# A gate projection split into four groups and placed inside the attention loop of a fused linear-attention layer on Trainium2

## The reference

```python
xn = _layernorm(x, axis=-1)                      # per token, 2048 features
q, k, v = xn @ Wq + bq, xn @ Wk + bk, xn @ Wv + bv
qf, kf = elu(q) + 1, elu(k) + 1                  # 16 heads of 128
# chunks of 128 tokens: kv and ksum of all earlier chunks are a running state
out = (qf @ kv_state + causal(qf @ kf.T) @ v) / (z_inter + z_intra + EPS)
s = out @ Wo + bo
g = silu(_layernorm(xn) @ ternary(W))            # the "f" projection
y = x + s * g
```

## Time and profile before

| what | us |
|---|---|
| runs shown | 4029.22 and 4381.51, median 4205.36 |
| the profiled execution | 4017.58 |
| its span, first to last instruction (core 3) | 4016.1 |
| PE busy | 2907.0 (72%) |
| DVE busy | 1137.6 (28%) |
| ACT busy | 1035.4 (26%) |

### The profile page before, as it was taken

One profiled execution on the slowest core, in us unless ns is written; L12 is line 12 of the kernel. 1 busy time (PEld: TensorE's weight loads), 2 busy tenths in 40 slices (PEclk: granted clock), 3 DMA queues, 4 the chain that ended last, 5 costly groups with the idle time before them and its releaser, 6 DMA issues.

```text
span 4016.1 us, 43354 instructions; the slowest of 8 cores (3976.9 to 4016.1 us)
## 1 busy us (share of the span) xinstructions
PE 2907.0 (72%) x15876; PEld 1535.7 (38%) x15876; DVE 1137.6 (28%) x1469; ACT 1035.4 (26%) x1200; POOL 218.6 (5%) x268
## 2 busy tenths in 40 slices
PE   1244545686969598777969597768959696859876
PEld 1011112443453344434444345434444345334443
DVE  4222363313231322313140322232141323232222
ACT  2010101412333132313232133313241233313221
POOL 2233112000000000000000000000000000000000
PEclk8676767797979698788979798879979797979888
DMA  5888867154404542254404542254404541344223
GB/s 190 273 290 283 295 227 243 40 154 170 152 31 128 171 152 95 63 158 165 152 22 138 172 153 71 89 174 152 131 30 150 178 153 37 123 134 152 95 79 129
DMA packets 225227, 581.81 MB, mean 145 GB/s; under 512 B 26240, under 2 KB 26336, under 8 KB 200448
## 3 DMA queue, kind: packets, MB, share of 16 engines
q1 hardware_dynamic: 198144, 436.30, 34.7%
q0 software_dynamic: 26880, 142.74, 10.1%
HBM read 503.43 MB, written 75.50 MB: 144 GB/s over the span
## 4 chain that ended last, share of the span: by engine, by line
PE 60%; DMA 13%; DVE 11%; issue 8%; ACT 5%; POOL 1%; DVEq 0%; SPq 0%; ACTq 0%; POOLq 0%
PE psA L492 51%; DMA wsc<-pcast 6%; DVE xn2T L455 3%; DMA y<-xres 3%; DMA wring<-wsc 3%; DVE kvbf L661 2%; ACT scr L634 2%; ACT scr L639 2%; DMA xres<-x 1%; PE psB L608 1%; PE psB L431 1%; PE psB L614 1%; PE psB L437 1%; PE psA L580 1%; DVE lst L349 1%
## 5 line engine op out<-in xcount | busy, mean ns | idle before, releaser
L492 PE MATMUL psA<-xnT,wring 128*128 128x512 bf16 x6144 | 1435.5, 399 | 381.5 <-DMA wring<-wsc 341.7
L492 PEld LDWEIGHTS psA<-xnT,wring 128*128 128x128 bf16 x6144 | 621.1, 102 | 1193.5 <-issue 538.8
L492 PE MATMUL psA<-xn2T,wring 128*128 128x512 bf16 x2048 | 478.3, 399 | 113.6 <-DVE ksumst L675 63.9
L492 PE MATMUL psA<-qat,wring 128*128 128x512 bf16 x2048 | 443.3, 379 | 0.0
L492 PEld LDWEIGHTS psA<-xn2T,wring 128*128 128x128 bf16 x2048 | 207.3, 102 | 382.1 <-issue 163.3
L723 DVE TENSOR_TENSOR xnT<-scr,vg 128x512 bf16<-128x512 f32 x128 | 88.6, 692 | 805.3 <-ACT scr L715 805.3
L492 PEld LDWEIGHTS psA<-qat,wring 128*128 128x128 bf16 x2048 | 200.4, 98 | 241.6
L431 PE MATMUL psB<-identb_s,xns 128*128 128x128 bf16 x512 | 59.7, 310 | 231.1 <-DVE xn2T L455 137.2
L507 ACT ACTIVATE scr<-psA,bs_q 128x512 f32<-128x512 f32 x128 | 88.0, 687 | 488.0 <-PE psA L492 482.4
L516 DVE SCALAR_TENSOR_TENSOR qat<-scr 128x512 bf16<-128x512 f32 x128 | 88.6, 692 | 418.5 <-ACT scr L510 418.5
L536 ACT ACTIVATE vg<-psA,bs_v 128x512 bf16<-128x512 f32 x128 | 88.0, 687 | 452.8 <-PE psA L492 452.8
(11 more groups left out here) (97 smaller groups left out, 2529.2 us busy)
## 6 DMA issues: line engine op xcount, KB each, us to landing
wring<-wsc SPq DMA_DIRECT2D x1280, 256.0 KB, 2.7
wsc<-pcast POOLq DMA_DIRECT2D x160, 256.0 KB, 8.1
xln<-x POOLq DMA_DIRECT2D x32, 1024.0 KB, 7.2
xres<-w_f SPq DMA_DIRECT2D x32, 1024.0 KB, 6.5
xres<-x POOLq DMA_DIRECT2D x32, 1024.0 KB, 8.1
y<-xres POOLq DMA_DIRECT2D x32, 1024.0 KB, 7.2
xres<-w_q SPq DMA_DIRECT2D x16, 1024.0 KB, 7.5
xres<-w_k SPq DMA_DIRECT2D x16, 1024.0 KB, 7.6
```

The lines of the kernel that those rows point to most:

```text
L492: op("tensor", lambda e, k=k, ti=ti, bk=bk, rb=rhs_buf: e.matmul(psA[:, bk * 512:(bk + 1) * 512], wring[k % NRING][:, (ti % 8) * 128:(ti % ...
```

## The change

The body of `proj_phase` becomes `proj_tile`, and the f projection is no longer a stage of its own: tiles 4j to 4j+3 are computed at the end of chunk j of the attention loop. As `vg` still holds v there, Silu writes the gate into `xnT`, and the product of stage 6 goes from `xnT` into `vg`. Layer norm A of the next super-chunk now stands behind the last f tile. No instruction is added or removed in the code.

```diff
+            def proj_tile(m, to, evac_fn, rhs_buf, rhs_deps):
...
             def proj_phase(m, evac_fn, rhs_buf, rhs_deps):
                 for to in range(NT):
+                    proj_tile(m, to, evac_fn, rhs_buf, rhs_deps)
...
+            def evac_f(to, bk, pe_n):
+                wait("scalar", s_pe, pe_n)
+                op("scalar", lambda e, to=to, bk=bk: e.activation(
+                    xnT[:, to * T:(to + 1) * T], psA[:, bk * 512:(bk + 1) * 512],
+                    AF.Silu), [(s_ac, 1)])
+                psA_bank_rel[bk] = (s_ac, s_ac.n)
...
                 set_rel("a_m", (s_pe, pe_io))
+                for to in range(4 * j, 4 * j + 4):
+                    proj_tile("f", to, evac_f, xn2T,
+                              [(s_ac, ac_ln_done)])
+            f_done_ac = s_ac.n
             attn_dv_done = s_dv.n
...
             if sc + 1 < nsc:
                 emit_ln_A(sc + 1, attn_dv_done)
-
-            def evac_f(to, bk, pe_n):
-                wait("scalar", s_pe, pe_n)
-                op("scalar", lambda e, to=to, bk=bk: e.activation(
-                    vg[:, to * T:(to + 1) * T], psA[:, bk * 512:(bk + 1) * 512],
-                    AF.Silu), [(s_ac, 1)])
-                psA_bank_rel[bk] = (s_ac, s_ac.n)
-
-            proj_phase("f", evac_f, xn2T, [(s_ac, ac_ln_done)])
-            f_done_ac = s_ac.n
...
                 op("vector", lambda e, to=to, ssl=ssl: e.tensor_tensor(
-                    xnT[:, to * T:(to + 1) * T], scr[:, ssl[0]:ssl[1]],
-                    vg[:, to * T:(to + 1) * T], ALU.mult), [(s_dv, 1)])
+                    vg[:, to * T:(to + 1) * T], scr[:, ssl[0]:ssl[1]],
+                    xnT[:, to * T:(to + 1) * T], ALU.mult), [(s_dv, 1)])
...
-                        xnT[:, t * T + j * 128: t * T + (j + 1) * 128],
+                        vg[:, t * T + j * 128: t * T + (j + 1) * 128],
...
-            set_rel("xnT", (s_pe, s_pe.n))
+            set_rel("xnT", (s_dv, sg_dv_done))
+            set_rel("vg_next", (s_pe, s_pe.n))
```

More of the change, by code:

```diff
@@ L467, in build_nc @@
             dv_ln_done, ac_ln_done = emit_ln_B(sc)
+            def proj_tile(m, to, evac_fn, rhs_buf, rhs_deps):
+                kA, wnA = stream_whalf(m, to, 0)
+                kB, wnB = stream_whalf(m, to, 1)
+                bk = to % 4
+                r0 = psA_bank_rel[bk]
+                if r0 is not None:
+                    wait("tensor", r0[0], r0[1])
+                if to == 0:
+                    for sem, cnt in rhs_deps:
+                        wait("tensor", sem, cnt)
+                wait("tensor", wnA[0], wnA[1])
+                for ti in range(NT):
+                    k = kA if ti < 8 else kB
+                    incs = []
+                    if ti == 0 and pending_wfree[0]:
+                        incs = [(s_wfree, pending_wfree[0])]
+                        pending_wfree[0] = 0
+                    if ti == 8:
+                        incs = [(s_wfree, 1)]
+                        wait("tensor", wnB[0], wnB[1])
+                    if ti == NT - 1:
+                        incs = [(s_pe, 1)]
+                    op("tensor", lambda e, k=k, ti=ti, bk=bk, rb=rhs_buf: e.matmul(
+                        psA[:, bk * 512:(bk + 1) * 512],
+                        wring[k % NRING][:, (ti % 8) * 128:(ti % 8 + 1) * 128],
+                        rb[:, ti * T:(ti + 1) * T],
+                        start=(ti == 0), stop=(ti == NT - 1)), incs)
+                pending_wfree[0] += 1
+                evac_fn(to, bk, s_pe.n)
+                pump(2)
@@ L469, in proj_phase @@
             def proj_phase(m, evac_fn, rhs_buf, rhs_deps):
                 for to in range(NT):
[L471 to L496, removed]
@@ L497, in proj_phase @@
-                    pending_wfree[0] += 1
-                    evac_fn(to, bk, s_pe.n)
-                    pump(2)
+                    proj_tile(m, to, evac_fn, rhs_buf, rhs_deps)
             def mk_evac_qk(dst, bias_key):
@@ L729, in build_nc @@
             proj_phase("o", evac_o, qat, [(s_dv, attn_dv_done)])
+            sg_dv_done = s_dv.n
             for j in range(NCH):
```

## The result

| | before | changed |
|---|---|---|
| profiled execution, us | 4017.58 | 4131.86 |
| its span (slowest core), us | 4016.1 | 4130.3 |
| median of all runs, us | 4303.33 (8 runs) | 4134.69 (9 runs) |
| ratio, with 95% interval | | 1.0277 (1.0259 to 1.0295) |

Most executions of the kernel before took 6 to 10% longer than its others, so the medians can't be set against each other and the ratio is taken over the shorter ones alone. The forecast was 4150 us with a range of 4085 to 4215 and a ratio of 1.033 to the profiled execution. Against the profiled execution, which the forecast was meant for, direction and range held. The growth came out at 114 us, where the sum had 132. (Set against the median of 4205.36 that was shown at first, 4150 would read as 1.3% faster, the wrong way.)

A forecast was written before the change was run, and what follows sets the result against it. From super-chunk 1 on, PE and what stops it set the time. Per super-chunk 5.0 + 3.9 + 6.2 + 1.6 = 16.7 us, seven times, plus 15.1, gave 132 on 4017.6: 4150 us, range 4085 to 4215.

The forecast's parts named there:

- the sum: All terms together: 16.7 us in each of seven super-chunks and 15.1 in the last, 132 us more.
- That the f groups would fill no halt: Ahead of f in each chunk: f needs psA, so PE still idles 8.04 us before each of 32 groups.
- The rival that they fill it: f groups start right behind the key-value product, filling halts of 8.04 us, 257 us in all: 3893 us; chance 0.03.
- Layer norm A moving to o: Its stall moves behind o's fourth tile: o 11.3 us longer, f 9.7 shorter, 1.6 us more per super-chunk.
- The rival of an o without a stall: ACT finds time for layer norm A beside the last f group, so o does not stall: 4071 us; chance 0.07.
- The f groups: Each of four groups restarts at the lower clock and takes 15.88 us: 6.2 us more per super-chunk.
- The tables: Ln of chunks 1 to 3 follows a Silu and needs a table load of 1.30 us: 3.9 us per super-chunk.
- four of the first kind make 88.56 us, 5.0 us more: Attention chunks with transposes in the open, as chunk 0 had them: 22.14 us each, 88.56 against 83.53 per super-chunk.
- The rival of the kept clock: f groups between chunks keep TensorE at 2.4 GHz, granted clock 1.00 at each group's start: 4018 us; chance 0.09.

The follow-up runs named there:

- e4: The changed kernel with VectorE freeing psA first, bank by bank, and scaling the outputs into qat only afterwards; ratio 0.9868 to the kernel before.
- e6: The changed kernel with the next chunk's 32 transposes done once more ahead of the f group, as filler thrown away; ratio 1.0241 to the kernel before.
- e1: The changed kernel with Identity in place of Silu, so no table is switched (timing only); ratio 1.0220 to the kernel before.
- e3: The changed kernel with a one-column Ln behind the copy of vtok in chunks 1 to 3, loading Ln's table early; ratio 1.0234 to the kernel before.
- e11: The changed kernel with the next chunk's transposes and copies ahead of each f group and a one-column Ln behind its Silus; ratio 1.0017 to the kernel before.
- e10: The changed kernel with psA freed first, bank by bank, and a one-column Ln loading Ln's table early; ratio 0.9692 to the kernel before.
- e2: The changed kernel with the next chunk's k and v transposes and their copies moved ahead of the f group; ratio 1.0041 to the kernel before.

## What of the prediction held, and which step failed

**That the f groups would fill no halt: right.** 32 halts of about 8 us, all released by VectorE. The rival that they fill it (3893 us) is out; e4 shows that `psA` was what held them, since with `psA` freed first the halt is 1.65 us. (The prediction looked for 8.04 us each; they measure 7.1 to 8.2.)

**Layer norm A moving to o: right.** Predicted +79 us in o, measured +77.0, with PE going on 23.03 us after o begins (22.95 predicted). The rival of an o without a stall is out.

**The f groups: right.** Predicted 15.88 us each, measured 510.8 us for 32, 15.96 each. The prediction called the cause the restart at the lower clock level. The granted clock of 0.50 at the start of each group shows it, and so does e6: the groups that start at 1.00 take 13.8 us.

**The tables: right in kind and price.** e1 took out 35.1 us where 40 were expected, e3 28.5 of 31.

**Attention: the step that failed.** The step was "four of the first kind make 88.56 us, 5.0 us more", and with the tables 8.9 us per super-chunk, 71 in all. Measured are 53 us: the parts of the four chunks ahead of f take 722.2 us in all against 669.2. The mechanism was right, the size a third too large, and these 18 us are the whole distance from 132 to 114. The mean of chunk 1 is 23.12 us, of chunk 3 23.06, of chunk 2 22.27, where the step had 23.44 for each; chunk 0 has 21.83, not 22.14. One half of it is the chunk itself: in e1, with no load anywhere, chunks 1 to 3 take 21.8 to 21.9 us in nearly every case, where the step had 22.14. The other half is chunk 2, which in four of eight super-chunks took 21.51 us with the load in it. The output matmuls (L618 and L624 in turn) are paced by the clock; in chunk 1 of super-chunk 3:

```profile
2093.48 0.27 PE L618 MATMUL psB<-qat,kvbf 128*128 128x128 bf16 x1 [2.46 <-ACT vtok L580]
2093.54 0.31 PE L624 MATMUL psB<-a_m,vtok 128*128 128x128 bf16 x1
2093.65 0.31 PE L618 MATMUL psB<-qat,kvbf 128*128 128x128 bf16 x1
```

and in chunk 2:

```profile
2131.69 0.22 PE L618 MATMUL psB<-qat,kvbf 128*128 128x128 bf16 x1 [2.46 <-ACT vtok L580]
2131.75 0.22 PE L624 MATMUL psB<-a_m,vtok 128*128 128x128 bf16 x1
2131.80 0.22 PE L618 MATMUL psB<-qat,kvbf 128*128 128x128 bf16 x1
```

The matmuls follow each other 0.11 us apart in the one and 0.05 in the other, at granted clocks of 0.50 and 1.00, with the same halt of 2.46 us ahead. The prediction took one chunk's duration as fixed, and it has two values, 1.6 us apart. The rival of the kept clock was thus right in a small part and wrong as a whole: its own test, a granted clock of 1.00 at the start of each group, gave 0.50 in all 32.

**What the sum could not show.** The terms held for the change, but they don't add for its mends. Undoing the transposes alone was worth 100 us where my account had 32. A table load saved was worth 1.2 us per place in e3, 0.7 in e11 and 3.1 in e10 (means of the cores). Each edit shortens or lengthens a halt of PE, and in these traces the clock of what follows changed with it. The change lost little by this, but of the mends only e1 and e3 came out near their estimates from single terms; e2 and e10 were off by a factor of more than two.

Left open: why chunk 2 keeps the high clock in half of the super-chunks and chunk 1 in none, why the same filler lifts the clock in some places and not in others, and the extra 6 to 10 us of e5.

## What to carry to other kernels

Work moved into an engine's halt helps only if it needs nothing that the halt waits for. Look at which buffer the moved work writes and who frees it, and free that one first; here an earlier, bank-wise release by VectorE was worth 171 us, more than the 114 that the place of the matmuls had cost. When work goes into a loop, count what follows it around: the waits in front of it, the table switches on ScalarE, the restarts of TensorE and the chain that used to stand behind it are each paid once per turn.

## What the runs showed of the hardware that was not expected

- Transposes can lift TensorE's clock, though not reliably. In the lines of e6 PE stands for 3.01 us, the 32 filler transposes run from 2066.62 for 3.2 us, the granted clock rises from 0.50 to 1.00 at 2069.38 while they run, and f takes 13.8 us. That came in 113 of 192 places. Behind an unbroken halt of 7 to 8 us it came in none, and f takes 15.1 to 16.8 us on the slowest core.
- A halt of 1.65 us ahead of f did not prevent a slow f: 16.4 to 16.6 us in e4, where a halt of 3.49 us stood ahead of the product before it, and 15.4 us in e10, where that one was 2.21. What counts is not the last halt alone.
- A one-column activation is enough to have a table loaded early: the 1.28 us load and 0.20 us for the column, both in time in which ScalarE waited.
